# A four-layer graph network in one kernel: a one-word GpSimd memset ahead of each gather of the sum passes

## What is computed

```python
# layer 0: three iterations of edge attention (4 heads), feed-forward, GRU
# layer 1 (GIN): once
agg = jax.ops.segment_sum(jax.nn.relu(x[src]), dst, num_segments=N)
h = relu(batch_norm(((1 + eps) * x + agg) @ W1.T + b1)) @ W2.T + b2
# layer 2 (gated graph network): four steps; each edge has one of 4 types
for _ in range(4):
    m = segment_sum((h[src] @ W_edge[type].T + b_edge[type]), dst)
    h = gru(m, h)
# layer 3: graph transformer (8 heads), batch norm, feed-forward
```

## Time and profile before

| | us |
|---|---|
| median of 3 runs | 12465.03 |
| lowest, highest | 12452.8, 12473.96 |
| profiled execution: span from the first to the last instruction | 12433.7 |
| the five sum passes (windows of the trace) | 919, 921, 920, 919, 918 |

### The profile page before, as it was taken

The page is one execution under the profiler, slowest core; times in us unless marked ns, Lnnn a source line. Parts: engine busy times, 40 slices in busy tenths (PEclk is TensorE's granted clock), DMA queues, the critical chain, the costliest instruction groups (busy, mean ns, idle before and its releaser), DMA issues. The chain is left out here.

```text
span 12433.7 us, 154586 instructions
## 1 busy us (share of the span) xinstructions
PE 6625.2 (53%) x36192; PEld 5643.9 (45%) x36193; DVE 4969.4 (40%) x11746; ACT 2217.8 (18%) x4249; POOL 6378.4 (51%) x6364
## 2 busy tenths in 40 slices
PE   4555687555687555686334333533533343355555
PEld 3555674555574555674333232333323333334443
DVE  4444664444674444673223221322312232235555
ACT  1222453222453222452000000000000000011111
POOL 2555432555432555431664566366366636625553
PEclk6777898777798777797556665655755575577777
DMA  2333321333331333330111211111111111112221
GB/s 78 112 113 114 101 85 51 113 111 113 97 90 47 113 113 115 99 89 20 45 45 32 72 45 45 57 45 45 53 50 45 44 59 45 45 39 78 77 77 56
DMA packets 698397, 893.93 MB, mean 72 GB/s; under 512 B 148418, under 2 KB 443212, under 8 KB 698131
## 3 DMA queue, kind: packets, MB, share of 16 engines
q0 software_dynamic: 198368, 429.61, 13.5%
q1 hardware_dynamic: 498474, 461.96, 11.8%
q10 hardware_dynamic: 1416, 0.86, 0.0%
HBM read 698.72 MB, written 193.14 MB: 72 GB/s over the span
## 5 line engine op out<-in xcount | busy, mean ns | idle before, releaser
L851 POOL DMA_INDIRECT l_sums_ring<-table_typed,tile_idx x2512 | 2482.8, 988 | 1773.3 <-issue 727.3
L960 PE MATMUL psum<-l_sums_ring,select 128*128 x7840 | 1669.2, 393 | 3039.8 <-DVE acc L941 1086.8
L821 POOL DMA_INDIRECT acc<-table_x,index x2016 | 2045.3, 1015 | 2166.5 <-DVE index L816 1541.0
L960 PEld LDWEIGHTS psum<-l_sums_ring,select 128*128 128x128 f32 x7840 | 1513.3, 293 | 3198.5 <-issue 3195.3
L941 DVE TENSOR_TENSOR acc<-acc,psum 128x128 f32 x980 | 280.5, 286 | 3179.6 <-remote 2414.8
L1078 PE MATMUL psum<-ident,select 128*128 128x128 f32 x2016 | 435.4, 355 | 1493.1 <-ACT l_scores_mixT L1018 507.6
L1053 DVE TENSOR_TENSOR acc<-l_scores_key,psum 128x512 f32<-128x512 f32 x504 | 345.9, 686 | 1776.8 <-ACT l_scores_key L1026 1331.8
L1078 PEld LDWEIGHTS psum<-ident,select 128*128 128x128 f32 x2016 | 295.5, 180 | 1569.1 <-issue 947.7
L821 POOL DMA_INDIRECT l_pass_ring<-table_kv,index x672 | 675.5, 1005 | 635.5 <-issue 264.4
L851 POOL DMA_INDIRECT l_sums_ring<-table_x,tile_idx x628 | 618.2, 984 | 634.6 <-ACTq L78 335.0
L925 DVE SCALAR_TENSOR_TENSOR select<-dst_all,pair_start,iota_row 128x512 f32<-128x512 f32 x980 | 732.5, 748 | 524.8 <-issue 407.9
(11 more groups left out here) (343 smaller groups left out, 10753.4 us busy)
## 6 DMA issues: line engine op xcount, KB each, us to landing
acc<-in_edge_attr_dram SPq DMA_DIRECT2D x2016, 64.0 KB
rows_dram<-l_scores_mixT SPq DMA_DIRECT2D x504, 256.0 KB
l_values_ring<-rows_dram SPq DMA_DIRECT2D x504, 256.0 KB
table_typed<-l_rows_rows SPq DMA_DIRECT2D x40, 1024.0 KB, 4.3
l_sums_ring<-table_typed,tile_idx POOLq DMA_INDIRECT x2512
acc<-table_x,index POOLq DMA_INDIRECT x2016
l_pass_ring<-table_kv,index POOLq DMA_INDIRECT x672
table_x<-l_rows_rows SPq DMA_DIRECT2D x40, 256.0 KB, 2.3
```

What stands on the lines that cost most here:

```text
L821: pool.indirect_dma_start(out=ring[:, at, u, :], out_offset=None, in_=table, in_offset=bass.IndirectOffsetOnAxis(ap=index[:, at % REGIONS, ...
L851: pool.indirect_dma_start(out=ring[:, k % TILE_RING, u, :], out_offset=None, in_=table, in_offset=at).then_inc(gathered[k % REGIONS], 16)
L960: ins = pe.matmul(sums(k), select[:, k, u, :], rows, start=u == 0, stop=u == GROUP - 1)
```

## The change

Before each gather of a sum pass GpSimd writes the constant 0.0 to one column of `t1` (one word on each of 128 partitions). Each of the 628 gathers of a pass has its own column. The write counts no semaphore up, and nothing reads it.

```diff
@@ gathers_by_tile @@
                 for u in range(GROUP):
+                    pool.memset(t1[:, k * GROUP + u:k * GROUP + u + 1], 0.0)
                     at = bass.IndirectOffsetOnAxis(ap=tile_idx[:, k * GROUP + u:k * GROUP + u + 1], axis=0)
                     pool.indirect_dma_start(out=ring[:, k % TILE_RING, u, :], out_offset=None, in_=table, in_offset=at
                                             ).then_inc(gathered[k % REGIONS], 16)
```

## The result

| | before | with the memsets |
|---|---|---|
| median, us | 12465.99 | 12489.72 |
| lowest, highest | 12438.24, 12482.95 | 12464.69, 12518.46 |
| executions | 20 | 20 |
| profiled span | 12433.7 | 12490.2 |

A forecast was written before the change was run, and what follows sets the result against it. The sum passes were taken as bound by POOL's 1.25 us gather beat plus some 40 full-ring stalls a pass. Adding 3140 memsets at 0.10 us, 314 us, to 12465 gave 12779 us; range 12250 to 12970.

The forecast's parts named there:

- the one term of the sum: In the sum passes, 3140 one-word memsets between gathers at 0.10 us each add 314 us, 63 us a pass.
- the lower end: Least price of the memsets between gathers, if overlapped as at program start: 0.03 us each, 94 us in all.
- is counted as idle but is not free time: On POOL after each gather, 0.30 us pass with nothing to wait for, making a gather cost 1.25 us.
- A gain below the lower end would need the stalls to change: In the sum passes, memsets were held to add at least 94 us unless POOL's full-ring waits changed.
- The gathers' stretching: In the sum passes, a memset would be lengthened as gathers are now and then: 0.004 us each, 13 us in all.
- POOL starts again a fixed time later: At a full ring, POOL's stops stay as they are; a slower beat doesn't shorten them unless the consumers gain.
- The product that the add at 7108.38 wants: In a sum pass, DVE's add after 12.44 us of idling was taken to want a product recorded by 7098.24.
- the 31 us between the median and the profiled span: For the whole kernel, the median lies 31 us over the profiled span; this was carried into the forecast.
- The stalls take it in: Rival: consumers set a sum pass's length, so POOL's 491 us of waits absorb the memsets; 12465 us, chance 0.12.
- The sums come sooner: Rival: wider gaps between gathers release late sums and end 491 us of stalls; 12288 us, chance 0.21.
- The memset has a gap of its own: Rival: 0.30 us also passes ahead of each memset between gathers, 0.40 us each; 1256 us, 13721 in all, chance 0.10.
- Changing loads code: Rival: each gather after a memset pays 5.67 us for the switch of instruction; 17804 us, 30269 in all, chance 0.01.

## Why the prediction was wrong

**The step that failed is the one term of the sum**, "I take 0.10 us, the recorded duration of a memset of exactly this shape", with its bounds of 0.03 and 0.16. The duration was right (116 ns), and what it puts between two gathers is 0.00 us, below the lower end and below the 0.03 that I had named as the sign of a wrong price. The error is in the sentence on the gap ahead of it: that the 0.30 us "is counted as idle but is not free time". It is not free for a gather. For a memset half of it is free. I had no row that shows the one without the other, and took "the next gather can't start yet" for "POOL can do nothing". "A gain below the lower end would need the stalls to change" went wrong in the same way: the true lower end was nothing.

**The gathers' stretching** at 0.004 us each was in the right order for a nil. Beside one-word memsets the gathers of the changed kernel are even shorter (980 and 978 ns against 988 and 984). Most of the longer writes do stretch them, by some 14 ns on average with 128 words; 512 words at every gather do not.

**"POOL starts again a fixed time later"** holds, and it too takes the memset in: from the end of a wait to the gather 0.77 us passed in the median before and 0.80 after, 0.03 us later, which over 158 to 179 stops is some 5 us.

**Two readings of mine were off without moving the number.** The product that the add at 7108.38 wants is not the one recorded by 7098.24. DVE is one select ahead, so that one is the next pair's; the wanted one had ended at 7090.66, and the sum was 17.7 us late. And the 31 us between the median and the profiled span are no overhead to be carried: the profiled run of the changed kernel took 12492.1 us with a span of 12490.2, 1.9 more. The profile of the kernel before is of one of its quicker executions.

**The rival "The stalls take it in"** gave 12465 with a chance of 0.12. Its number nearly came out, but by luck: nothing was there to be taken in. Its mechanism holds all the same. With 128 words and with 512 once in a region POOL has 59 and 82 us more to do in a pass (294 and 408 in five), and the passes keep their length. So even had the memset cost its 0.10 us (63 a pass), nearly all of it would have been lost in the 98 us of slack. The argument that I set against it, that POOL at full beat loses what it loses for good, is refuted by the earlier trace rows set beside the pass of 922 us with 128 words. Both of my mistakes pushed the same way, and either one put right would have led to 12465.

**The rival "The sums come sooner"** is right that gathers further apart can end the late sums, and wrong for this change. The gap did not grow, so nothing could be relieved; at a gap of 0.38 us there is no relief (sums late by 2777 us against 2673), and at 0.70 at every gather it is whole. There the cost of 395 ns a gather exceeds it.

**"The memset has a gap of its own" and "Changing loads code"** are refuted by the first timeline: no gap ahead of the memset, and a gather behind one that takes 0.95 us, 947 ns in the median as before. The 6.62 us of a pass's first gather are there with the memset as without it. The Trainium skill (GPSIMD Engine Reference, section 2.1, Instruction dispatch) says that one Pool instruction does not hold back the next, which each core of the engine begins when its share is done. The trace agrees as far as the memset starts with the gather's recorded end (7110.91); the measured price is 0.00 us, less than the lower end of 0.03 to which I had put this rule, and what the single cores do the profile doesn't show.

**What the 24 us are is not settled.** They appear on chips with stalls (1.0016, 1.002) and not on one without (0.9995), so they don't come from the beat; the later restart explains some 5 of them. The first pair of profiles has 21 more stops and 64 us more idling in them, but the second profile of the change has only 10 and 8 more than the kernel before, so the stops don't settle it; the sums are late by 2673 us before and by 2686 and 2641 in the two profiles of the change. One memset in a region costs some 9 us there, too little to be told from either. Nor does any run tell what holds the sums back: the trace shows a product ended at 7111.76, its increment of `p_summed` recorded at 7130.56 and its add at 7130.69, but not what delays the increment, nor why it happens on some chips only. A ring of another size, or a wait of POOL for each region before the next, which would tell whether it is the number of gathers under way, was not run. Nor was 256 words on a chip with stalls, which would tell at what gap between 0.38 and 0.70 us the relief sets in.

## What to carry to other kernels

Before pricing an instruction by its duration, ask whether the idle time beside it can hold it: a gap after each instruction of a queue may be closed to its own kind and open to others, and a probe of two lengths finds the free part. Where a full ring stops the engine that is slowed, look at what sets the time of the release; if that is not the engine itself, its slowing is taken in up to the slack (here an estimated 98 us a pass, of which up to 82 were tried and taken in). And take the kernel before along on every chip: here the same edit, 128 words, is 2.8% slower on one and 0.1% on another.

## What the runs showed of the hardware that was not expected

- Indirect gathers of 128 rows of 512 bytes start every 1.25 us; 0.15 us of the 0.305 us between them take a memset by GpSimd for nothing, and a gather starts no sooner than some 0.155 us (0.151 to 0.162) after the memset.
- A memset by GpSimd takes 0.12 us for one word on each of 128 partitions, 0.22 for 128 words, 0.33 for 256 and 0.54 for 512; four one-word memsets in a row take 0.20 us together.
- The kernel before took 10622 to 10627 us on three chips and 12378 to 12466 wherever its sums came late. There TensorE's sums release DVE's adds only after up to 21 us of idling while gathers follow each other with gaps of 0.30 to 0.38 us, also with 0.70 at every fourth, and none is late with 0.70 at every gather. What is late is the increment of TensorE's semaphore as the trace records it: 18.8 us after its product's recorded end in one case, with the next one 0.09 us behind.
